# Mamba gates from tanh of the halved argument, one stage of its convolved rows a state earlier on VectorE, and a router threshold found two bits a round

## What is computed

```
# mamba, per sequence (xn = normalised x; 256 inner channels, 16 states)
u, res = split(xn @ W_in + b_in)
u      = silu(causal_conv4(u) + conv_b)          # gate 1
dt, B, C = split(u @ W_x)                        # 64, 16, 16
delta  = softplus(dt @ W_dt + b_dt)
h_t    = exp(delta*A) * h_{t-1} + delta*u*B ;  y = sum_n h*C + u*D
x      = x + (y * silu(res)) @ W_out + b_out     # gate 2
# experts with capacity: 4096 tokens, 8 experts, top 2, 768 places an expert
prio   = where(chosen, weight, -1); keep the 768 largest prio of each expert
```

## Time and profile before

| | |
|---|---|
| median of 3 runs | 3293.44 us |
| profiled execution | 3296.06 us, span 3294.0 us |
| busy share of the span | PE 69%, DVE 61%, ACT 39%, POOL 35% |
| mamba's scans | 2235.3 to 2847.4 us |
| last router's 30 rounds | 2933.0 to 3001.6 us |
| first slice of the span | DMA 221 GB/s |

### The profile page before, as it was taken

One profiled execution on the slowest core, in us unless ns is written; L12 is line 12 of the kernel. 1 busy time (PEld: TensorE's weight loads), 2 busy tenths in 40 slices (PEclk: granted clock), 3 DMA queues, 4 the chain that ended last, 5 costly groups with the idle time before them and its releaser, 6 DMA issues. The chain is left out here.

```text
span 3294.0 us, 47377 instructions
## 1 busy us (share of the span) xinstructions
PE 2262.0 (69%) x15091; PEld 1545.8 (47%) x15091; DVE 2016.8 (61%) x5443; ACT 1298.1 (39%) x2671; POOL 1152.8 (35%) x1205
## 2 busy tenths in 40 slices
PE   2899999999653457309468986757888888640190
PEld 0566666666542346207335553645555555430170
DVE  3677777777545956401455664767888888655016
ACT  1445445445242013103124543327777777310030
POOL 3244234234000000364321111017777777502551
PEclk9899999999876569559767888878999999855595
DMA  7200000000100000022232232000000000000122
GB/s 221 75 1 0 0 0 0 0 0 0 58 0 0 0 0 0 9 60 58 79 77 64 70 76 78 0 0 1 0 0 0 0 0 0 0 0 15 52 61 78
DMA packets 105709, 93.66 MB, mean 28 GB/s; under 512 B 12252, under 2 KB 92150, under 8 KB 105462
## 3 DMA queue, kind: packets, MB, share of 16 engines
q1 hardware_dynamic: 97942, 76.78, 8.5%
q0 software_dynamic: 7680, 15.81, 1.5%
HBM read 62.08 MB, written 46.26 MB: 33 GB/s over the span
## 5 line engine op out<-in xcount | busy, mean ns | idle before, releaser
L2621 POOL TENSOR_SCALAR mb_w<-mb_duT,mb_bT 128x256 f32<-128x256 f32 x512 | 463.8, 924 | 144.9 <-PE bank L2631 133.6
L2557 DVE TENSOR_TENSOR_SCAN mb_hs<-mb_dA,bank 128x512 f32<-128x512 f32 x256 | 300.6, 1203 | 31.3 <-issue 24.6
L38 POOL TENSOR_TENSOR scrap<-ones 128x1 f32<-128x1 f32 x96 | 19.9, 207 | 817.7 <-DVE gla_ss L419 487.1
L2650 PE MATMUL bank<-mb_hc,ident 128*128 128x512 f32 x512 | 251.6, 614 | 24.5 <-DVE mb_hc L2567 23.3
L1901 DVE TENSOR_REDUCE ra_mx<-bank 128x2 f32<-128x512 f32 x256 | 166.8, 687 | 103.3 <-PE bank L1778 101.6
L2612 ACT ACTIVATE mb_dA<-mb_delta,mb_A 128x255 f32<-128x255 f32 x512 | 217.6, 494 | 3.6 <-DVE mb_hs L2557 3.4
L1987 ACT ACTIVATE ra_pT<-bank 128x512 f32<-128x512 f32 x256 | 139.6, 596 | 132.7 <-PE bank L1798 131.6
L1552 ACT ACTIVATE e_hid<-bank,e_b 128x512 f32<-128x512 f32 (+1 forms) x128 | 81.1, 634 | 236.6 <-PE bank L1571 233.5
L2631 PE MATMUL bank<-ident,mb_w 128*128 128x128 f32 x1024 | 149.5, 279 | 35.6 <-DVE mb_hs L2557 26.2
L1535 POOL DMA_INDIRECT results<-e_y,e_x x112 | 107.2, 957 | 146.4 <-DVE e_y L1606 121.4
L1563 PE MATMUL bank<-ident,e_x 128*128 128x128 f32 x112 | 18.8, 292 | 197.9 <-DMA e_x<-queue 197.9
(11 more groups left out here) (511 smaller groups left out, 6225.6 us busy)
## 6 DMA issues: line engine op xcount, KB each, us to landing
results<-const_empty SPq DMA_DIRECT2D x2, 4096.0 KB
e_got<-results SPq DMA_DIRECT2D x32, 256.0 KB, 3.3
rope_rows<-ra_part SPq DMA_DIRECT2D x48, 128.0 KB, 1.9
ra_k<-rope_rows SPq DMA_DIRECT2D x32, 192.0 KB, 3.2
ra_q<-rope_rows SPq DMA_DIRECT2D x32, 192.0 KB, 4.3
queue<-const_spare_rows SPq DMA_DIRECT2D x1, 4128.0 KB
e_x<-queue SPq DMA_DIRECT2D x8, 516.0 KB
e_w<-in_L_ffn_w SPq DMA_DIRECT2D x2, 2048.0 KB, 8.2
```

The lines of the kernel that those rows point to most:

```text
L2557: dve.tensor_tensor_scan(hs[n // 2 % 2][:, n % 2, :, :].rearrange("p c t -> p (c t)"), dA[n % RD][:, :, :].rearrange("p c t -> p (c t)"), ...
L2621: ins = pool.tensor_scalar(w[n % RH][:, h, :], duT[k][:, h, :], bT[k][:, h, n:n + 1], None, ALU.mult)
L2650: ins = pe.matmul(YB[:, :], g.ident[:, :], hc[grp % 2][:, j, :, :].rearrange("p c t -> p (c t)"), start=(n == 0), stop=(n == NS - 1))
```

## The change

- **Gates.** silu(v) = (v/2) * (1 + tanh(v/2)). ScalarE writes `cv` and `rs` halved (scale 0.5 and a bias `half_b`, halved once by two small VectorE instructions), then one Tanh. VectorE's multiply becomes a scalar_tensor_tensor, (t + 1) * v, of the same shape. Each gate loses two ScalarE functions.
- **Order.** `mb_uc` moves from after n = 6 to after n = 5, `mb_rest` from n = 8 to n = 7; ScalarE's two copies move from n = 7 to n = 6. TensorE's order is as before.
- **Router.** `val` is transposed once by TensorE so that a partition holds 256 values of one expert (16 partitions an expert). 15 rounds then each try three candidates: three compares over 128x256 with a running sum (`accum_out`), one f32 matmul with a constant 128x128 matrix `same_expert`, and the number kept of the three picks the two bits. At the end a transpose turns the threshold back. `same_expert` (64 KB) is one more transfer at the start of the program.

```diff
@@ router
-                    dve.tensor_tensor(cand[:, :], prefix[:, :], bit[:, :], ALU.bitwise_or).then_inc(done, 1)
+                    dve.tensor_tensor(cand[:, :], prefix[:, 0:1].broadcast_to([P, CANDS]), unit[:, :],
+                                      ALU.bitwise_or).then_inc(done, 1)
                     after(1)
-                    dve.tensor_tensor(hit[:, :, :], val[:, :, :], per_expert(cand[:, :].bitcast(F32)), ALU.is_ge)\
-                        .then_inc(done, 1)
...
-                        dve.tensor_reduce(hits[:, :], hit[:, :, :].rearrange("p t e -> p e t"), AXX, ALU.add)\
-                            .then_inc(hit_ready, 1)
...
+                    for j in range(CANDS):
+                        ins = dve.tensor_scalar(seen[:, j, :], by_expert[:, :], cand[:, j:j + 1].bitcast(F32), 0.0,
+                                                ALU.is_ge, ALU.add, accum_out=counts[:, j:j + 1])
+                    ins.then_inc(hit_ready, 1)
+
+                    dve.tensor_scalar(unit[:, :], unit[:, :], 2, None, ALU.logical_shift_right).then_inc(done, 1)
                     dve.wait_ge(cnt_psum, b + 1)
...
+                    after(3)
+                    dve.tensor_scalar(worth[:, :], worth[:, :], 0.25, None, ALU.mult).then_inc(done, 1)
...
+                        dve.tensor_reduce(gain[:, :], keep[:, :], AXX, ALU.add).then_inc(done, 1)
                     after(5)
-                    dve.tensor_tensor(prefix[:, :], prefix[:, :], keep[:, :], ALU.bitwise_or).then_inc(done, 1)
+                    dve.tensor_tensor(prefix[:, :], prefix[:, :], gain[:, :], ALU.bitwise_or).then_inc(done, 1)
...
+                pe.wait_ge(val_ready, 1)
+                for h in range(2):
+                    ins = pe.transpose(cnt_bank[:, h * P:(h + 1) * P], flat(a3[4])[:, h * P:(h + 1) * P],
+                                       g.ident[:, :])
...
+                    pe.matmul(tot_bank[:, 0:CANDS], g.same_expert[:, :], counts[:, :], start=True, stop=True)\
                         .then_inc(cnt_psum, 1)
@@ mamba
-            dve.tensor_tensor(uc[k][:, :, :], cv[:, :, :], e1[:, :, :], ALU.mult).then_inc(uc_ready, 1)
+            dve.scalar_tensor_tensor(out=uc[k][:, :, :], in0=e1[:, :, :], scalar=1.0, in1=cv[:, :, :],
+                                     op0=ALU.add, op1=ALU.mult).then_inc(uc_ready, 1)
-                ins = act.activation(cv[:, c, :], UB[:, c * 256:(c + 1) * 256], ACT.Identity, bias=conv_all[:, c:c + 1])
+                ins = act.activation(cv[:, c, :], UB[:, c * 256:(c + 1) * 256], ACT.Identity, bias=half_b[:, c:c + 1],
+                                     scale=0.5)
-            act.activation(e1[:, :, :], cv[:, :, :], ACT.Exp, scale=-1.0).then_inc(e_ready, 1)
+            act.activation(e1[:, :, :], cv[:, :, :], ACT.Tanh).then_inc(rc_ready, 1)
...
-    DVE_WHEN = {6: (4,), 8: (5,), 9: (7,), 10: (6,)}
-    ACT_WHEN = {1: (0,), 3: (1, 2), 4: (3,), 7: (4,), 8: (5,), 9: (6,), 11: (8, 9)}
+    DVE_WHEN = {5: (4,), 7: (5,), 9: (7,), 10: (6,)}
+    ACT_WHEN = {1: (0,), 3: (1, 2), 6: (4,), 8: (5,), 9: (6,), 11: (8, 9)}
     PE_WHEN = {0: (0,), 1: (1,), 2: (2,), 6: (4,), 7: (5,), 8: (7,), 9: (9,), 11: (6,)}
```

More of the change, by code:

```diff
@@ L1248, in router @@
     small = [sb(f"s{k}", [P, E_N]) for k in range(4)]
-    bit, prefix, cand, keep = [sb(f"i{k}", [P, E_N], I32) for k in range(4)]
-    worth = sb("worth", [P, E_N])
-    hits, ones = sb("hits", [P, E_N], BF16), sb("ones", [P, P], BF16)
+    unit, cand, keep = sb("unit", [P, CANDS], I32), sb("cand", [P, CANDS], I32), sb("keep", [P, CANDS])
+    prefix, gain = sb("prefix", [P, 1], I32), sb("gain", [P, 1], I32)
+    worth, counts = sb("worth", [P, CANDS]), sb("counts", [P, CANDS])
+    by_expert, seen, limit = sb("by_expert", [P, 2 * P]), sb("seen", [P, CANDS, 2 * P]), sb("limit", [P, E_N])
+    val_ready, turned_psum, found, limit_psum = sig("val"), sig("turned"), sig("found"), sig("limitp")
     base = sb("base", [P, E_N])
@@ L1331, in _ @@
                 step(dve.tensor_tensor(tmp[:, :, :], oh2[:, :, :], per_tile(w2), ALU.mult))
[L1332 to L1337, removed]
+                dve.tensor_tensor(val[:, :, :], val[:, :, :], tmp[:, :, :], ALU.add).then_inc(val_ready, 1)
@@ L1358, in _ @@
+                    with nc.allow_low_precision(reason="up to three times a power of two is exact"):
+                        dve.tensor_reduce(gain[:, :], keep[:, :], AXX, ALU.add).then_inc(done, 1)
                     after(5)
-                    dve.tensor_tensor(prefix[:, :], prefix[:, :], keep[:, :], ALU.bitwise_or).then_inc(done, 1)
+                    dve.tensor_tensor(prefix[:, :], prefix[:, :], gain[:, :], ALU.bitwise_or).then_inc(done, 1)
                     after(6)
-                n[0] = so_far + BITS * PER_BIT
@@ L1362, in _ @@
-                thr = per_expert(prefix[:, :].bitcast(F32))
+                n[0] = so_far + STEPS * PER_STEP
+                dve.tensor_copy(small[0][:, 0:1], g.zeros[:, 0:1]).then_inc(found, 1)
+                dve.wait_ge(limit_psum, 1)
+                step(dve.tensor_copy(limit[:, :], cnt_bank[:, 0:E_N]))
+                thr = per_expert(limit[:, :])
                 step(dve.tensor_tensor(over[:, :, :], val[:, :, :], thr, ALU.is_gt))
@@ L1466, in _ @@
             if by_weight:
-                with pe.Fori(0, BITS) as b:
+                pe.wait_ge(val_ready, 1)
+                for h in range(2):
+                    ins = pe.transpose(cnt_bank[:, h * P:(h + 1) * P], flat(a3[4])[:, h * P:(h + 1) * P],
+                                       g.ident[:, :])
+                ins.then_inc(turned_psum, 1)
+                with pe.Fori(0, STEPS) as b:
                     pe.wait_ge(hit_ready, b + 1)
-                    pe.matmul(cnt_bank[:, 0:E_N], ones[:, :], hits[:, :], start=True, stop=True)\
+                    pe.matmul(tot_bank[:, 0:CANDS], g.same_expert[:, :], counts[:, :], start=True, stop=True)\
                         .then_inc(cnt_psum, 1)
+                pe.wait_ge(found, 1)
+                pe.transpose(cnt_bank[:, 0:P], prefix[:, 0:1].bitcast(F32).broadcast_to([P, P]), g.ident[:, :])\
+                    .then_inc(limit_psum, 1)
             pe.wait_ge(oh_ready, 1)
```

66 lines of the change are left out of this document (29 added, 37 removed).

## The result

The changed kernel is slower: 3300.43 us against 3293.05 us (medians of 20 runs each), a ratio of 1.0023 with a 95% interval of 1.0016 to 1.0030. The forecast was 3257.3 us, range 3238 to 3277. The profiled execution spans 3298.8 us, 4.8 us more than before.

| part | forecast | traces |
|---|---|---|
| load, to the first layer's first statistics | +0.3 | +0.4 |
| mamba, start | -3.6 | -3.5 |
| mamba, first to last scan | -17.3 | +30.3 |
| last router | -15.5 | -20.6 |
| the rest of the program | 0 | -1.8 |

What follows compares the result with a forecast made beforehand. It took TensorE and VectorE as near their limit in mamba, and a chain of dependent VectorE steps in the last router. Terms -17.3 - 3.6 - 15.5 + 0.3 = -36.1 us gave 3257.3 us, range 3238 to 3277.

Steps and rivals of the forecast that it cites:

- `mb_rest`: Mamba, each sequence: it would wait about 1.9 us for ScalarE's copies, leaving 0.1 of the 2.74 us saved before `mb_uc`.
- load, to the first layer's first statistics: Program start: 64 KB more to load before the first layer, at 221 GB/s, 0.3 us longer.
- mamba, start: Ahead of sequence 0: one Tanh ends 3.88 us sooner, less 0.3 us of VectorE preamble, net 3.6 us saved.
- mamba, first to last scan: Mamba's steady state: 1.15 us saved in each of 15 sequences, 17.3 us in all.
- last router: Last router: 15 rounds of 3.45 us replace 30 of 2.301 us; 17.2 less 1.7 us, 15.5 us saved.
- the first one on mamba's steady state: Mamba, each sequence: VectorE reaches `mb_uc` after one scan with the gate ready, so its 2.74 us wait goes.
- `mb_delta`: Mamba, each sequence: softplus's log ends at 2457.3, before VectorE arrives at 2457.4, so the 1.14 us wait goes.
- the counts: Router round: three compares with a running sum take 1.43 us, bounds 0.72 and 2.0 us.
- the hand-over: Router round: from the counts through TensorE's f32 matmul to its reader, 0.80 us.
- the edges: Around the router's loop: transposes and copies before and after it cost 1.7 us.
- its two bounds: Forecast's own range, 3244 to 3271 us: bounds of the router's three-count time, and 0.5 to 1.8 us a mamba sequence.
- the starving one: Rival in mamba: early `mb_rest` waits 5.0 us and starves TensorE, 3.1 us lost a sequence, 3303.8 us; chance 0.04.

Runs made afterwards that it cites:

- experiment 1: Changed kernel with the gated output `yy` in `az` instead of `uc` and without `mb_uc`'s wait for the output product: 3256.17 us, ratio 0.9876 to the kernel before.
- experiment 2: Changed kernel with `yy` in `az` but `mb_uc`'s wait for the output product kept: 3305.78 us, ratio 1.0034 to the kernel before.
- experiment 7: Kernel before with only the new places of `mb_uc`, `mb_rest` and ScalarE's copies, old gates and old router: 3380.31 us, ratio 1.0258.
- experiment 6: Changed kernel with `mb_uc` back after scan 6 and `mb_rest` still after scan 7: 3255.39 us, ratio 0.9879 to the kernel before.
- experiment 4: Changed kernel with the old places of `mb_uc`, `mb_rest` and ScalarE's copies, Tanh gates and new router kept: 3251.16 us, ratio 0.9861 to the kernel before.

## Why the prediction was wrong

The step that failed is the first one on mamba's steady state: "In the new place VectorE gets to `mb_uc` after one scan ... No wait is left: 2.74 us go." I looked for the arrival of the operands (rows, gate) and left out the other condition of the same instruction, that its destination be free. The profile of before names for a wait only the releaser that came last, so its list of waits could not show this one; the code did, and its time stood in TensorE's rows. The new place moves VectorE's arrival from 2444.84 to 2442.5, ahead of an output product that ends at 2445.6.

Point by point:

- *`mb_uc`*: forecast 0, measured 3.09 us (experiments 1 and 2 turn it off and on). It costs 2.34 us a sequence at full clock (39.91 against 37.57 us), less than 3.09 us because the 0.71 us before scan 7 in experiment 1 are covered by it, and 1.05 us more by TensorE's lower clock behind it. The split rests on the first full sequence, the one at full clock; experiment 2 has the same 39.91 us there. 14 x 2.34 + 13 x 1.05 = 46.4 us of the 47.9 us between the changed kernel and experiment 1.
- *`mb_rest`*: the reasoning was right (the W_x product comes out of TensorE's queue); 1.62 us where the kernel is as I thought it, with the product 1.94 us behind the start of the sum, 1.93 us before. Behind the missed wait it is 1.81 us at full clock and 2.88 us at the lower clock. For the clock I had no step, neither here nor in experiment 7, where the same wait grows to 4.40 us.
- *`mb_delta`*: forecast 1.14 us to 0; it went to 0.28 us.
- *Steady state without the missed wait*: forecast -17.3 us, measured -17.6 us. The mechanism was right for a kernel that was not the one changed; that the sum fits so closely is in part luck. Twelve sequences gain 1.06 us each and not 1.15, the two that ran at the lower clock in the kernel before gain 1.85 us each, the first, from its first scan on, gains 2.9 us, and the end behind the last `mb_rest` loses 1.8 us.
- *Start*: -3.6 forecast, -3.5 measured. *Load*: +0.3, +0.4.
- *Router*: -15.5 forecast, -20.6 measured in the trace and -19.1 by itself. All terms had the right sign; the counts (1.28 for 1.43 us), the hand-over (0.69 for 0.80 us) and the edges (0.9 for 1.7 us) were each priced too high.
- *Range*: 3244 to 3271 us is narrower than what its two bounds give when they are added, 3237 to 3276 us. It doesn't touch the failed step.
- *Rivals*: the starving one gave 3303.8 us, near the time measured, but by another mechanism: its wait of `mb_rest` was to be 4.3 us or more and was 2.88 us, and experiment 6 has the early `mb_rest` and loses 4.2 us. A time that fits is no proof of its cause. The chance of 0.94 for faster came from counting rivals among the waits that the profile names, and none for a wait that it hides.

## What to carry to other kernels

Before an instruction is moved ahead, write down every condition it waits for, operands and destination, and read from the trace when each is met: the wait list names only the last one, and once that is gone the next is the price. If a buffer is reused under another name (`yy = uc`), its last reader may stand far back in another engine's queue. A wait ahead of a recurrence holds the engine that feeds the next hand-over as well, so it adds to the next wait instead of using it up, and here the lower clock that came behind it made the next wait longer still. And where a result is late because an engine reaches it out of its queue, try its place there first, since here two numbers in TensorE's order were worth 76 us (3300.43 to 3224.46).

## What the runs showed of the hardware

TensorE's clock was granted at the 1.2 GHz level for 3.4 us a sequence in the changed kernel (2448.7 to 2452.1; windows of one us read 0.50 from 2449 to 2452). It fell near the end of the 1.50 us that TensorE stood idle after a busy stretch; the sum behind it took 3.06 us instead of 1.88. In experiment 7 TensorE stood idle for 3.37 us, and windows of one us read 0.50 from 2480 to 2486. It is no fixed answer to the idle time: behind 1.50 us of it in the first full sequence (2285.83) the sum took 1.98 us, and experiment 4 has both with one order; there the clock fell at 2412.5, 1.5 us after the 1.74 us of idle time had ended. What decides stays open. A count by `accum_out` over 128x256 f32 on VectorE took 475 ns and its read 82 ns (45 of each), overlapping so that three take 1.28 us, where the compare without a sum takes 294 ns.
